# The end of a mixture-of-experts program: waits, gathers and loads behind the last expert

## The chip, the core and the metric

One core of a Trainium2 chip. The time is the device time of one launch in microseconds, the median of three runs. TensorE (PE) does the matmuls, VectorE (DVE) and ScalarE (ACT) the elementwise work, GpSimd (POOL) issues the indirect DMAs and those that add to memory, SyncE (SP) issues the plain loads and stores. Each engine works through its own list of instructions; they meet through semaphores, counters in which a DMA counts 16 when all its data has landed.

## The reference

With x of shape (2, 4096, 512):

```
xn  = layernorm(x)
out = x + attention(xn) + experts(xn)

attention: q, k, v = split(xn @ W_qkv + b_qkv), 16 heads of 32; relu on q and k; both weighted by the cosine and
           the sine of the position; linear attention through k^T v, divided by its norm; then @ W_out + b_out
experts:   probs = softmax(xn @ choice_w^T)                  # 8 experts
           G, I = top_k(probs of each expert, 1024 tokens)   # per batch
           h = silu(xn[I] @ w1[e]);  y = G * (h @ w2[e]);  rows I of the output += y
```

Each of the 8 experts takes 1024 tokens of each of the 2 batches, with w1[e] 512x1024 and w2[e] 1024x512.

## The kernel before

Matmuls are done at more than the plain precision: each operand is split into a high and a low part, and one product is three matmuls (hi·hi, hi·lo, lo·hi; lines 1291 to 1293). The first 960 us or so are the layer norm, attention and routing. They store the normed rows and the router's chances to a scratch tensor in HBM, and write x + bias + attention into the output there.

The rest is the expert stage, and the change is in it alone. It runs over 8 experts (E) and in each over 4 units (UNITS) of 512 token rows, two units for each batch. For a unit:

- GpSimd gathers the rows of the unit to come with 16 indirect DMAs (line 449) and its gains with 4 (line 455), as soon as VectorE has transposed the rows of the present one (`rows_turned`).
- VectorE transposes the rows (line 907), ScalarE takes the high part (`rows_hi`, line 583), VectorE the low part (`rows_lo`, line 914).
- TensorE does the up projection in 8 parts, ScalarE applies silu (line 748), VectorE splits the result (lines 1259 and 1261); then the down projection in 4 tiles of 128 rows. ScalarE scales each tile by the gain into `y` (line 767), and GpSimd scatters it, an indirect DMA that adds 128 rows to the output in HBM (line 546). It counts up `added[b]`.
- ScalarE must not overwrite `y` before the previous unit's scatters have landed. At a unit inside an expert it waits on `added` itself. At the first unit of an expert it waits on `expert_added`, which GpSimd counts up at the end of its loop body, after its own wait for all scatters of batch 1 (lines 551 and 552).
- The weights of the next expert are loaded by SyncE into one raw buffer for w1 (line 357, 4 DMAs) and one for w2 (line 362), each when the split of the present one is done. The split of w1 for the next expert (ScalarE line 579, VectorE line 899) sits in the last unit.
- The token lists of an expert and batch are made by VectorE and TensorE two units ahead; GpSimd copies a new list into `idx`, which the scatters use, at units 1 and 3 (`copy_list`).

`apart(eng)` (line 297) puts a no-op between a wait and the instruction behind it, so that the wait isn't taken into that instruction. GpSimd, SyncE and TensorE run the experts in a hardware loop (`Fori`), in which the values waited for are in registers; ScalarE and VectorE have them written out. All this looks one unit and one expert ahead without an exception at the end: in the eighth expert, w1 and w2 of expert 0 are loaded again, w1 is split again, and in the last unit the rows and gains of unit 0 are gathered, transposed and split again, and `copy_list(0)` runs. Nothing uses them. Behind the loops SyncE waits for those loads and for all stores and scatters, and GpSimd for its scatters and for those gathers (line 553). The Block around the five lists then ends each with a DRAIN and releases them together (in the profile these instructions have line 126).

Of the kernel before, what the change touches and what calls it, by code (L numbers as in the profile page):

```python
# [33 lines left out]
B, L, D = 2, 4096, 512  # L34
H, HD = 16, 32
E, F = 8, 1024
# [3 lines left out]
HPG = P // HD  # L40
KF = F // P
BLK = 512
TPB = BLK // P
# [5 lines left out]
UNITS = B * CAP // BLK  # L49
HALVES = CAP // BLK  # L50
SLOT_TILES = CAP // P
# [6 lines left out]
AHEAD, DMA_AHEAD = 1, 16  # L58
# [60 lines left out]
def build(nc, x, w_qkv, b_qkv, w_out, b_out, choice_w, w1, w2, consts, bits, out, scratch):  # L119
# [6 lines left out]
    with ExitStack() as ctx:  # L126
        def sem(name):
            return ctx.enter_context(nc.semaphore(name))
# [159 lines left out]
        rows_turned, xi_hi_ready, xi_ready = sem("gtr_done"), sem("xi_hi_ready"), sem("xi_ready")  # L288
        up_done, silu_done, h_ready = sem("up_done"), sem("silu_done"), sem("h_ready")
        down_done, y_ready = sem("down_done"), sem("y_ready")  # L290
        added, expert_added = [sem(f"added{b}") for b in range(B)], sem("expert_added")

        block = ctx.enter_context(nc.Block())

        def apart(eng):

            eng.nop(nofuse=True)
# [8 lines left out]
        def _(sp):  # L306

            for signal in (mm_done, kv_done, vv_ready, q_read, k_read, v_read, lg_read, o_raw, otr_done, out_done, fin, list_pe, idx_ready,
                           silu_done, h_ready, down_done, y_ready, expert_added):
                sp.sem_inc(signal, AHEAD)  # L310
            sp.sem_inc(prob_stored, DMA_AHEAD)
            def store_normed(j, s):
# [42 lines left out]
            def load_w1(e):  # L355
                for i in range(HPG):
                    sp.dma_start(w1_raw[i * HD:(i + 1) * HD, :, :],
                                 w1[bass.ds(e, 1), i * P:(i + 1) * P, :].rearrange("e (k p) f -> p (e k) f", p=HD)
                                 ).then_inc(w1_in, 16)

            def load_w2(e):
                sp.dma_start(w2_raw[:, :, :], w2[bass.ds(e, 1), :, :].rearrange("e (k p) d -> p (e k) d", p=P)
                             ).then_inc(w2_in, 16)

            for b in range(B):
# [10 lines left out]
                n = b * NBLK  # L376
# [33 lines left out]
                    sp.wait_ge(q_ready, B * NT)  # L410
                    load_w2(0)

            with sp.Fori(0, E) as e:
                nxt_e = (e + 1) % E
                sp.wait_ge(w1_ready, (e + 1) * KF)
                load_w1(nxt_e)
                sp.wait_ge(w2_ready, (e + 1) * KF)
                load_w2(nxt_e)
            sp.wait_ge(w1_in, HPG * 16 * (E + 1))
            sp.wait_ge(w2_in, 16 * (E + 1))  # L420
            for s in range(2):
                sp.wait_ge(xn_stored[s], 16 * B * NBLK)
            for s in range(RES):
# [7 lines left out]
        def _(pool):  # L431
# [88 lines left out]
            for s in range(RES):  # L520
                pool.wait_ge(out_stored[s], 16 * B * NT // RES)
            pool.wait_ge(prob_stored, DMA_AHEAD + 16 * B)
            with pool.Fori(0, E) as e:
                for u in range(UNITS):
                    b = u // HALVES
                    pool.wait_ge(y_ready, AHEAD + e * (UNITS * TPB) + u * TPB)
                    if u % HALVES == 0:
                        pool.wait_ge(idx_copied, e * B + (b + 1))
                    if u == 1:

                        pool.wait_ge(idx_ready, AHEAD + e * B + 2)
                        apart(pool)
                        copy_list(1)
                    elif u == UNITS - 1:
                        pool.wait_ge(idx_ready, AHEAD + e * B + 3)
                        pool.wait_ge(added[0], (e + 1) * (16 * SLOT_TILES))
                        apart(pool)
                        copy_list(0)
                    pool.wait_ge(rows_turned, (e * UNITS + u + 1) * TPB)
                    apart(pool)  # L540
                    gather((u + 1) % UNITS)

                    for tt in range(TPB):
                        pool.wait_ge(y_ready, AHEAD + e * (UNITS * TPB) + (u * TPB + tt + 1))
                        apart(pool)
                        nc.gpsimd.indirect_dma_start(  # L546
                            of[:, :], bass.IndirectOffsetOnAxis(ap=idx[:, u * TPB + tt:u * TPB + tt + 1], axis=0),
                            y[:, tt, :], None, compute_op=ALU.add).then_inc(added[b], 16)

                pool.wait_ge(added[B - 1], (e + 1) * (16 * SLOT_TILES))  # L550
                pool.sem_inc(expert_added, 1)
            for tt in range(TPB):
                pool.wait_ge(rows_in[tt], 64 * (E * UNITS + 1))
            pool.wait_ge(gain_in[0], 64 * (E * UNITS // 2 + 1))


        @block.scalar
        def _(act):
# [183 lines left out]
            for e in range(E):  # L742
                for u in range(UNITS):
                    n = e * UNITS + u
                    for m in range(KF):
                        act.wait_ge(up_done, n * KF + m + 1)
                        act.wait_ge(h_ready, AHEAD + n * KF + max(m - 1, 0))
                        nc.scalar.activation(hf[:, m % 2, :], ps[:, m % 2, :], ACT.Silu).then_inc(silu_done, 1)  # L748
                        if u == 0:
                            if m == 0:  # L750
                                act.wait_ge(w2_in, (e + 1) * 16)
                                act.wait_ge(down_done, AHEAD + n * TPB)
                            nc.scalar.copy(w2_hi[:, m, :], w2_raw[:, m, :]).then_inc(w2_hi_ready, 1)

                    if u == 0:
                        act.wait_ge(expert_added, AHEAD + e)
                    else:
                        before = u - 1
                        act.wait_ge(added[before // HALVES],
                                    (e * SLOT_TILES + (before % HALVES + 1) * TPB) * 16)  # L760
                    for tt in range(TPB):
                        rows_hi(n + 1, tt)
                        act.wait_ge(down_done, AHEAD + n * TPB + tt + 1)
                        if tt == 0:
                            act.wait_ge(gain_in[u % 2], e * (64 * UNITS // 2) + (u // 2 + 1) * 64)
                        apart(act)
                        nc.scalar.activation(y[:, tt, :], ps[:, 2 + tt % 2, :], ACT.Copy,  # L767
                                             scale=gain[:, u % 2, tt, bass.ds(e, 1)]).then_inc(y_ready, 1)
                        if u == UNITS - 1:
                            if tt == 0:  # L770
                                act.wait_ge(w1_in, (e + 2) * (HPG * 16))
                            for m in (2 * tt, 2 * tt + 1):
                                w1_high(m)
# [3 lines left out]
        def _(dve):  # L777
# [472 lines left out]
            for e in range(E):  # L1250
                for u in range(UNITS):
                    n = e * UNITS + u
                    made, of_b, turn = u % HALVES == 0, (u // HALVES + 1) % B, e * B + (u // HALVES + 1)
                    of_e = e + 1 if of_b == 0 else e
                    for m in range(KF):
                        dve.wait_ge(silu_done, AHEAD + n * KF + m + 1)
                        if m == 0:
                            dve.wait_ge(down_done, AHEAD + n * TPB)
                        me.did(nc.vector.tensor_copy(h_hi[:, m, :], hf[:, m % 2, :]))  # L1259
                        me.wait()  # L1260
                        nc.vector.tensor_tensor(h_lo[:, m, :], hf[:, m % 2, :], h_hi[:, m, :].bitcast(F32),  # L1261
                                                ALU.subtract).then_inc(h_ready, 1)
                        if u == 0:
                            dve.wait_ge(w2_hi_ready, e * KF + m + 1)
                            nc.vector.tensor_tensor(w2_lo[:, m, :], w2_raw[:, m, :], w2_hi[:, m, :].bitcast(F32),
                                                    ALU.subtract).then_inc(w2_ready, 1)
                        if made:
                            if m == 1:
                                list_head(of_e, of_b, turn)
                            elif 2 <= m <= 5:  # L1270
                                list_part(of_e, of_b, turn, m - 2, one_lo[:, m % 2, :, :])
                            elif m == KF - 1:
                                list_tail(of_b, turn, e * B + 1)
                    rows_turn(n + 1, 0)
                    for tt in range(TPB):
                        if tt < TPB - 1:
                            rows_turn(n + 1, tt + 1)
                        rows_lo(n + 1, tt)
                        if made and tt == 1:
                            list_rows(of_b, turn)  # L1280
                        if u == UNITS - 1:
                            for m in (2 * tt, 2 * tt + 1):
                                w1_low(m, e * KF + (KF + m + 1))

# [316 lines left out]
```

## Time and profile before

| | us |
|---|---|
| median of 3 runs (2411.46 to 2414.36) | 2411.73 |
| the profiled execution | 2411.47 |
| its span, first to last instruction | 2409.6 |
| busy in the span: TensorE | 2364.5 |
| VectorE | 1401.0 |
| GpSimd | 1106.8 |
| ScalarE | 839.1 |

Times in the profile are microseconds unless marked ns. A queue's own instructions (names that end in q: waits, branches, DRAIN) are not counted as busy. A matmul's end is modelled, and matmuls overlap, so a busy TensorE is not TensorE at its peak. What a DMA instruction shows as its time on GpSimd is the making of its descriptors; the data lands later, and "to landing" is counted from the start of the instruction. Behind a group in square brackets stands how long its engine was idle before it, and what ended that.

### The profile page before, as it was taken

How to read it: one execution, taken by the hardware profiler on the slowest of the kernel's cores; microseconds unless marked ns; L12 is line 12 of the kernel's file. 1: busy time of each engine (PE TensorE's matmuls, PEld its weight loads, DVE VectorE, ACT ScalarE, POOL GpSimd, SP SyncE). 2: the span in 40 equal slices, each digit the busy share in tenths (PEclk: the TensorE clock that was granted, in tenths of full speed). 3: DMA queues.
4: the chain of work that ended last, by engine and by line, in shares of the span. 5: the costliest groups of instructions: out<-in, count | busy, mean ns of one | idle time of the engine just before them, and what ended most of it. 6: DMA issues, size and time to landing. Idle time of an engine off the chain costs nothing.

```text
span 2409.6 us, 34867 instructions
## 1 busy us (share of the span) xinstructions
PE 2364.5 (98%) x12586; PEld 2006.1 (83%) x12586; DVE 1401.0 (58%) x2730; ACT 839.1 (35%) x1470; POOL 1106.8 (46%) x980
## 2 busy tenths in 40 slices
PE   7999999999999999999999999999999999999997
PEld 6899978888999888888888888888888888888886
DVE  7777788967776888643543543543543544444433
ACT  4455444444454445322322322322223223223222
POOL 2000024400000246666566665665665665765765
PEclk9999999999999999999999999999999999999998
DMA  7555433445453434622522522522523423423322
GB/s 189 168 120 157 121 61 53 56 95 161 121 146 99 76 55 70 152 51 45 121 48 46 119 47 45 120 45 48 120 44 53 116 44 64 104 46 72 94 44 44
DMA packets 128139, 209.66 MB, mean 87 GB/s; under 512 B 28728, under 2 KB 53944, under 8 KB 127808
## 3 DMA queue, kind: packets, MB, share of 16 engines
q0 software_dynamic: 57728, 119.09, 27.6%
q1 hardware_dynamic: 70336, 89.68, 12.9%
q8 instruction: 35, 0.57, 0.1%
q14 instruction: 40, 0.33, 0.0%
HBM read 124.54 MB, written 100.93 MB: 94 GB/s over the span
## 4 chain that ended last, share of the span: by engine, by line
PE 93%; DVE 5%; ACT 1%; issue 1%; DMA 1%; POOL 0%; SPq 0%; DVEq 0%; ACTq 0%; POOLq 0%
PE ps L1291 30%; PE ps L1292 29%; PE ps L1293 29%; PE ps L1387 2%; PE ps L1519 1%; PE ps L1318 1%; DVE work L1229 0%; DVE thr L1141 0%; DVE stats L785 0%; DVE work L1212 0%; DMA xo<-in_L_attn_x_dram 0%; DMA normed_rows<-xo 0%; DVE qT L1004 0%; PE ps L1505 0%; DVE xT_lo L846 0%
## 5 line engine op out<-in xcount | busy, mean ns | idle before, releaser
L449 POOL DMA_INDIRECT rows<-normed_rows,idx_row x528 | 563.7, 1068 | 209.0 <-issue 209.0
L1291 PE MATMUL ps<-xi_hi,w_hi 128*128 128x512 f32 x1024 | 404.3, 395 | 0.0
L1291 PE MATMUL ps<-w_hi,h_hi 128*128 128x512 f32 x1024 | 402.3, 393 | 0.0
L1292 PE MATMUL ps<-xi_lo,w_hi 128*128 128x512 f32 x1024 | 400.4, 391 | 0.0
L1292 PE MATMUL ps<-w_lo,h_hi 128*128 128x512 f32 x1024 | 399.4, 390 | 0.0
L1293 PE MATMUL ps<-w_hi,h_lo 128*128 128x512 f32 x1024 | 399.1, 390 | 0.0
L1293 PE MATMUL ps<-xi_hi,w_lo 128*128 128x512 f32 x1024 | 398.7, 389 | 0.0
L1259 DVE CAST h_hi<-hf 128x512 fp32r<-128x512 f32 x256 | 111.5, 436 | 411.2 <-ACT hf L748 410.9
L546 POOL DMA_INDIRECT out_dram<-y,idx x128 | 221.4, 1730 | 273.1 <-ACT y L767 260.3
L748 ACT ACTIVATE hf<-ps 128x512 f32<-128x512 f32 x256 | 153.1, 598 | 519.4 <-PE ps L1293 519.4
L1293 PE MATMUL ps<-wq_hi,xT_lo 128*128 128x256 f32 (+2 forms) x768 | 246.4, 321 | 0.0
L1291 PE MATMUL ps<-wq_hi,xT_hi 128*128 128x256 f32 (+2 forms) x768 | 246.4, 321 | 0.0
L767 ACT ACTIVATE y<-ps,gain 128x512 f32<-128x512 f32 x128 | 88.1, 689 | 453.6 <-PE ps L1293 453.6
L1292 PE MATMUL ps<-wq_lo,xT_hi 128*128 128x256 f32 (+2 forms) x768 | 245.6, 320 | 0.0
L1293 PEld LDWEIGHTS ps<-xi_hi,w_lo 128*128 128x128 f32 x1024 | 192.7, 188 | 41.0
L1293 PEld LDWEIGHTS ps<-w_hi,h_lo 128*128 128x128 f32 x1024 | 192.5, 188 | 40.5
L1291 PEld LDWEIGHTS ps<-w_hi,h_hi 128*128 128x128 f32 x1024 | 192.4, 188 | 39.1
L1291 PEld LDWEIGHTS ps<-xi_hi,w_hi 128*128 128x128 f32 x1024 | 192.3, 188 | 39.1
L1292 PEld LDWEIGHTS ps<-w_lo,h_hi 128*128 128x128 f32 x1024 | 192.5, 188 | 38.8
L1292 PEld LDWEIGHTS ps<-xi_lo,w_hi 128*128 128x128 f32 x1024 | 192.5, 188 | 38.0
L914 DVE TENSOR_TENSOR xi_lo<-rowsT,xi_hi 128x512 fp32r<-128x512 f32 x132 | 90.4, 685 | 220.0 <-ACT xi_hi L583 216.7
L1261 DVE TENSOR_TENSOR h_lo<-hf,h_hi 128x512 fp32r<-128x512 f32 x256 | 177.9, 695 | 8.8
(174 smaller groups left out, 4217.4 us busy)
## 6 DMA issues: line engine op xcount, KB each, us to landing
w_raw<-in_L_ffn_w_dram SPq DMA_DIRECT2D x36, 512.0 KB, 8.1
w_raw<-in_L_ffn_w_dram SPq DMA_DIRECT2D x9, 2048.0 KB, 9.1
xo<-in_L_attn_x_dram SPq DMA_DIRECT2D x32, 512.0 KB, 4.5
normed_rows<-xo SPq DMA_DIRECT2D x32, 512.0 KB, 4.7
out_dram<-bo POOLq DMA_DIRECT2D x16, 1024.0 KB, 9.2
out_dram<-xo POOLq DMA_DIRECT2D x64, 256.0 KB, 3.9
xn<-normed_rows SPq DMA_DIRECT2D x96, 128.0 KB, 2.4
rows<-normed_rows,idx_row POOLq DMA_INDIRECT x528, 2.6
```

The costliest lines, as they stand in the source:

```text
L449: nc.gpsimd.indirect_dma_start(rows[:, tt, a, :], None, pieces[:, :], bass.IndirectOffsetOnAxis(ap=idx_row[:, b, tile, a:a + 1], axis=0)). ...
L546: nc.gpsimd.indirect_dma_start(of[:, :], bass.IndirectOffsetOnAxis(ap=idx[:, u * TPB + tt:u * TPB + tt + 1], axis=0), y[:, tt, :], None, c ...
L748: nc.scalar.activation(hf[:, m % 2, :], ps[:, m % 2, :], ACT.Silu).then_inc(silu_done, 1)
L767: nc.scalar.activation(y[:, tt, :], ps[:, 2 + tt % 2, :], ACT.Copy, scale=gain[:, u % 2, tt, bass.ds(e, 1)]).then_inc(y_ready, 1)
L914: nc.vector.tensor_tensor(xi_lo[:, :, sl], rowsT[:, tt % 2, :, :], xi_hi[:, :, sl].bitcast(F32), ALU.subtract).then_inc(xi_ready, 1)
L1259: me.did(nc.vector.tensor_copy(h_hi[:, m, :], hf[:, m % 2, :]))
L1261: nc.vector.tensor_tensor(h_lo[:, m, :], hf[:, m % 2, :], h_hi[:, m, :].bitcast(F32), ALU.subtract).then_inc(h_ready, 1)
L1291: nc.tensor.matmul(dst, a_hi, b_hi, start=start, stop=False, skip_group_check=True)
L1292: nc.tensor.matmul(dst, a_hi, b_lo, start=False, stop=False, skip_group_check=True)
L1293: return nc.tensor.matmul(dst, a_lo, b_hi, start=False, stop=stop, skip_group_check=True)
L1318: last = nc.tensor.matmul(ps[:, 4, 16:32], one_lo[:, c % 2, j, :], pay[:, c * 8 + j, :], start=(c == 0 and j == 0), stop=(c == 3 and j == ...
L1387: last = nc.tensor.matmul(ps[:, i // 2, i % 2 * 4 * PW:(i % 2 + 1) * 4 * PW], kk[:, at:at + 2 * PW], vv[:, 2 * at:2 * at + 4 * PW], start= ...
```

## The change

The eighth expert gets exceptions, and one hand-over goes:

- SyncE loads no ninth pair of weights.
- GpSimd's loop runs over seven experts, and the eighth is written out behind it, with constants in its waits. In it the last unit has no `copy_list(0)` and no gathers, and its 16 scatters have no no-op between wait and DMA.
- GpSimd waits for scatters at no expert's end and not at the end of the program; `expert_added` is gone, and ScalarE waits on `added[1]` itself. SyncE's wait for all scatters stays.
- ScalarE and VectorE leave out the rows of unit 32 and the second split of expert 0's w1.

```diff
--- before.py
+++ after.py
@@ -288,7 +288,7 @@
         rows_turned, xi_hi_ready, xi_ready = sem("gtr_done"), sem("xi_hi_ready"), sem("xi_ready")
         up_done, silu_done, h_ready = sem("up_done"), sem("silu_done"), sem("h_ready")
         down_done, y_ready = sem("down_done"), sem("y_ready")
-        added, expert_added = [sem(f"added{b}") for b in range(B)], sem("expert_added")
+        added = [sem(f"added{b}") for b in range(B)]
 
         block = ctx.enter_context(nc.Block())
 
@@ -306,7 +306,7 @@
         def _(sp):
 
             for signal in (mm_done, kv_done, vv_ready, q_read, k_read, v_read, lg_read, o_raw, otr_done, out_done, fin, list_pe, idx_ready,
-                           silu_done, h_ready, down_done, y_ready, expert_added):
+                           silu_done, h_ready, down_done, y_ready):
                 sp.sem_inc(signal, AHEAD)
             sp.sem_inc(prob_stored, DMA_AHEAD)
             def store_normed(j, s):
@@ -410,14 +410,13 @@
                     sp.wait_ge(q_ready, B * NT)
                     load_w2(0)
 
-            with sp.Fori(0, E) as e:
-                nxt_e = (e + 1) % E
+            with sp.Fori(0, E - 1) as e:
                 sp.wait_ge(w1_ready, (e + 1) * KF)
-                load_w1(nxt_e)
+                load_w1(e + 1)
                 sp.wait_ge(w2_ready, (e + 1) * KF)
-                load_w2(nxt_e)
-            sp.wait_ge(w1_in, HPG * 16 * (E + 1))
-            sp.wait_ge(w2_in, 16 * (E + 1))
+                load_w2(e + 1)
+            sp.wait_ge(w1_in, HPG * 16 * E)
+            sp.wait_ge(w2_in, 16 * E)
             for s in range(2):
                 sp.wait_ge(xn_stored[s], 16 * B * NBLK)
             for s in range(RES):
@@ -520,7 +519,7 @@
             for s in range(RES):
                 pool.wait_ge(out_stored[s], 16 * B * NT // RES)
             pool.wait_ge(prob_stored, DMA_AHEAD + 16 * B)
-            with pool.Fori(0, E) as e:
+            def expert(e, last):
                 for u in range(UNITS):
                     b = u // HALVES
                     pool.wait_ge(y_ready, AHEAD + e * (UNITS * TPB) + u * TPB)
@@ -531,27 +530,27 @@
                         pool.wait_ge(idx_ready, AHEAD + e * B + 2)
                         apart(pool)
                         copy_list(1)
-                    elif u == UNITS - 1:
+                    elif u == UNITS - 1 and not last:
                         pool.wait_ge(idx_ready, AHEAD + e * B + 3)
                         pool.wait_ge(added[0], (e + 1) * (16 * SLOT_TILES))
                         apart(pool)
                         copy_list(0)
-                    pool.wait_ge(rows_turned, (e * UNITS + u + 1) * TPB)
-                    apart(pool)
-                    gather((u + 1) % UNITS)
+                    if u < UNITS - 1 or not last:
+                        pool.wait_ge(rows_turned, (e * UNITS + u + 1) * TPB)
+                        apart(pool)
+                        gather((u + 1) % UNITS)
 
                     for tt in range(TPB):
                         pool.wait_ge(y_ready, AHEAD + e * (UNITS * TPB) + (u * TPB + tt + 1))
-                        apart(pool)
+                        if not last:
+                            apart(pool)
                         nc.gpsimd.indirect_dma_start(
                             of[:, :], bass.IndirectOffsetOnAxis(ap=idx[:, u * TPB + tt:u * TPB + tt + 1], axis=0),
                             y[:, tt, :], None, compute_op=ALU.add).then_inc(added[b], 16)
 
-                pool.wait_ge(added[B - 1], (e + 1) * (16 * SLOT_TILES))
-                pool.sem_inc(expert_added, 1)
-            for tt in range(TPB):
-                pool.wait_ge(rows_in[tt], 64 * (E * UNITS + 1))
-            pool.wait_ge(gain_in[0], 64 * (E * UNITS // 2 + 1))
+            with pool.Fori(0, E - 1) as e:
+                expert(e, False)
+            expert(E - 1, True)
 
 
         @block.scalar
@@ -752,21 +751,22 @@
                                 act.wait_ge(down_done, AHEAD + n * TPB)
                             nc.scalar.copy(w2_hi[:, m, :], w2_raw[:, m, :]).then_inc(w2_hi_ready, 1)
 
-                    if u == 0:
-                        act.wait_ge(expert_added, AHEAD + e)
-                    else:
+                    if u == 0 and e > 0:
+                        act.wait_ge(added[B - 1], e * (16 * SLOT_TILES))
+                    elif u > 0:
                         before = u - 1
                         act.wait_ge(added[before // HALVES],
                                     (e * SLOT_TILES + (before % HALVES + 1) * TPB) * 16)
                     for tt in range(TPB):
-                        rows_hi(n + 1, tt)
+                        if n + 1 < E * UNITS:
+                            rows_hi(n + 1, tt)
                         act.wait_ge(down_done, AHEAD + n * TPB + tt + 1)
                         if tt == 0:
                             act.wait_ge(gain_in[u % 2], e * (64 * UNITS // 2) + (u // 2 + 1) * 64)
                         apart(act)
                         nc.scalar.activation(y[:, tt, :], ps[:, 2 + tt % 2, :], ACT.Copy,
                                              scale=gain[:, u % 2, tt, bass.ds(e, 1)]).then_inc(y_ready, 1)
-                        if u == UNITS - 1:
+                        if u == UNITS - 1 and e < E - 1:
                             if tt == 0:
                                 act.wait_ge(w1_in, (e + 2) * (HPG * 16))
                             for m in (2 * tt, 2 * tt + 1):
@@ -1271,14 +1271,17 @@
                                 list_part(of_e, of_b, turn, m - 2, one_lo[:, m % 2, :, :])
                             elif m == KF - 1:
                                 list_tail(of_b, turn, e * B + 1)
-                    rows_turn(n + 1, 0)
+                    more = n + 1 < E * UNITS
+                    if more:
+                        rows_turn(n + 1, 0)
                     for tt in range(TPB):
-                        if tt < TPB - 1:
+                        if more and tt < TPB - 1:
                             rows_turn(n + 1, tt + 1)
-                        rows_lo(n + 1, tt)
+                        if more:
+                            rows_lo(n + 1, tt)
                         if made and tt == 1:
                             list_rows(of_b, turn)
-                        if u == UNITS - 1:
+                        if u == UNITS - 1 and e < E - 1:
                             for m in (2 * tt, 2 * tt + 1):
                                 w1_low(m, e * KF + (KF + m + 1))
```

## Rows read from the trace of the kernel before

**Rows 1.** The page's part 4, the chain of waits by engine, share of the span.

```profile
PE 93%; DVE 5%; ACT 1%; issue 1%; DMA 1%; POOL 0%; SPq 0%; DVEq 0%; ACTq 0%; POOLq 0%
```

**Rows 2.** Windows, first and last expert: stretch, length, busy us (instructions), clock, DMA share, GB/s.

```profile
966.00:1144.00 178.00, 178.00 (x842) 145.81 (x841) 86.78 (x157) 47.13 (x79) 116.18 (x102) 1.00 0.38 80
...
2216.00:2395.00 179.00, 178.38 (x840) 146.05 (x838) 79.62 (x138) 47.48 (x81) 113.85 (x98) 1.00 0.36 72
```

**Rows 3.** Timeline after the last matmuls: start us, us, engine, line, operation [idle before <-releaser].

```profile
2393.99 0.39 PE L1293 MATMUL ps<-w_hi,h_lo 128*128 128x512 f32 x1
2394.47 0.69 ACT L767 ACTIVATE y<-ps,gain 128x512 f32<-128x512 f32 x1 [3.20 <-PE ps L1293]
2395.06 1.12 ACT L579 CAST w_hi<-w_raw 128x512 fp32r<-128x512 f32 x2
2395.70 1.29 DVE L899 TENSOR_TENSOR w_lo<-w_raw,w_hi 128x512 fp32r<-128x512 f32 x2 [3.54 <-ACT w_hi L579]
2395.92 1.90 POOL L546 DMA_INDIRECT out_dram<-y,idx  x1 [3.52 <-ACT y L767]
```

**Rows 4.** One source line, L126, queues' own instructions: ns min/median/max, first to last start.

```profile
L126 POOLq EVENT_SEMAPHORE  x2: 17/17/17, 2409.5 to 2409.5; - x2
...
L126 ACTq DRAIN  x1: 1672/1672/1672, 2394.5 to 2394.5; - x1
L126 DVEq DRAIN  x1: 814/814/814, 2396.2 to 2396.2; - x1
...
L126 POOLq DRAIN  x1: 7912/7912/7912, 2401.5 to 2401.5; - x1
```

**Rows 5.** Line L546 from 2395 us on: the last scatter's landing, from its issue.

```profile
DMA to landing us min/median/max: 5.0/5.0/5.0
```

**Rows 6.** Lines L427 (SyncE's last waits) and L553 (GpSimd's last wait).

```profile
L427 SPq EVENT_SEMAPHORE  x1: 28/28/28, 2400.9 to 2400.9; - x1
...
L553 POOLq EVENT_SEMAPHORE  x1: 43/43/43, 2401.2 to 2401.2; - x1
```

**Rows 7.** Windows: the end of the span after the landing (columns as in rows 2).

```profile
2400.90:2409.60 8.70, 0.00 (x0) 0.00 (x0) 0.00 (x0) 0.00 (x0) 0.00 (x0) 0.50 0.00 0
```

**Rows 8.** Line L1590, the start of the program, GpSimd (columns as in rows 4).

```profile
L1590 POOLq DRAIN  x1: 184/184/184, 0.3 to 0.3; - x1
...
L1590 POOL MEMSET const-uint8-127<- x1: 117/117/117, 0.3 to 0.3; 128x1 uint8 x1
```

**Rows 9.** Line L297, the no-op of apart(), on GpSimd's queue.

```profile
L297 POOLq EVENT_SEMAPHORE  x176: 17/17/17, 978.8 to 2395.2; - x176
```

**Rows 10.** Timeline of stage 2's end: ScalarE finishes a tile, GpSimd's DMA adds it.

```profile
971.25 0.59 ACT L738 COPY xo<-ps 128x512 f32<-128x512 f32 x1 [0.68 <-DMA out_dram<-xo]
...
972.13 0.90 POOL L502 DMA_DIRECT2D out_dram<-xo  x1 [1.78 <-ACT xo L738]
```

**Rows 11.** Lines L357 and L362, the loads of w1 and w2, SyncE's queue.

```profile
L357 SPq DMA_DIRECT2D w_raw<-in_L_ffn_w_dram x36: 311/317/686, 807.4 to 2221.2; - x36
...
L362 SPq DMA_DIRECT2D w_raw<-in_L_ffn_w_dram x9: 385/390/390, 961.4 to 2242.2; - x9
```

**Rows 12.** Timeline of GpSimd in the last unit.

```profile
2381.82 1.61 POOL L546 DMA_INDIRECT out_dram<-y,idx  x1 [0.30 <-issue]
2385.09 1.93 POOL L546 DMA_INDIRECT out_dram<-y,idx  x1 [1.66 <-ACT y L767]
```

**Rows 13.** Timeline of GpSimd where the seventh expert ends.

```profile
2218.36 1.89 POOL L546 DMA_INDIRECT out_dram<-y,idx  x1 [3.54 <-ACT y L767]
2227.47 1.96 POOL L449 DMA_INDIRECT rows<-normed_rows,idx_row  x1 [7.21 <-issue]
```

**Rows 14.** Line L546 from 2215 to 2229 us: that scatter's landing.

```profile
DMA to landing us min/median/max: 7.6/7.6/7.6
```

**Rows 15.** Timeline of VectorE, without and beside GpSimd's gathers.

```profile
2220.67 0.69 DVE L1261 TENSOR_TENSOR h_lo<-hf,h_hi 128x512 fp32r<-128x512 f32 x1
...
2228.91 0.69 DVE L1261 TENSOR_TENSOR h_lo<-hf,h_hi 128x512 fp32r<-128x512 f32 x1
```

## The prediction, made before the changed kernel was run

> **What bounds the kernel now.** I read the chain of waits first: 93% of the span is TensorE [rows 1]. Then the expert stage by expert, one stretch for each: in all eight TensorE is busy for the whole stretch (178.00 of 178.00 in the first, 178.38 of 179.00 in the last, which ends after TensorE does), at a granted clock of 1.00 [rows 2]. So nothing that another engine does in this stage is waited for by TensorE, and what the change can move lies behind the last matmul. I then read the end of the program by engine. The last recorded matmul runs to about 2394.4, ScalarE scales y from 2394.47 to 2395.16, GpSimd issues the last scatter from 2395.92 to 2397.82 [rows 3]. The span ends at 2409.6, 11.8 us later, with no engine busy. The queues' own instructions fill that tail. ScalarE's DRAIN starts at 2394.5 and ends at 2396.2, and VectorE's starts at 2396.2 and ends at 2397.0: both end with the last instruction of their engine. GpSimd's starts at 2401.5 and takes 7.912 us, to 2409.4; the semaphores that release all engines stand at 2409.5 [rows 4]. So the end is: last y, last scatter, its landing, GpSimd's waits, GpSimd's DRAIN. The landing is 5.0 us after the issue, at 2400.9 [rows 5]; at 2400.9 SyncE's wait on the same scatters is over too, and GpSimd's last wait, on gathers long landed, stands at 2401.2 [rows 6]. In the 8.7 us from 2400.90 on no DMA engine moves anything [rows 7]: the drain isn't waiting for data then, it takes 7.9 us of its own.
>
> **The change part by part.** The sum is made on the profiled execution, 2411.47 us with a span of 2409.6; the 1.9 us around the span stay. The median, 2411.73, lies 0.26 above it, and the gain is taken from the median.
>
> 1. GpSimd's wait for the last scatters, the increment behind it, the loop's last branch and the waits on the ninth expert's gathers go. Before, the drain starts at 2401.5; now its sequencer reaches it as soon as the scatter is handed over. What the drain then costs is not in the trace for this case (scatters in flight). Bounds: it needs its 7.9 us after GpSimd's own last instruction, or it needs all of them after the landing (gain only the 0.6 us of sequencer work between 2400.9 and 2401.5), or it costs next to nothing: the same engine's drain at the program's start, behind four memsets, took 184 ns and ended with them [rows 8]. With that last one SyncE's landing sets the end, and the gain is 2409.4 - 2400.9 = 8.5 us. I take the first. It is nearest to rows 4 and 8: no drain in the trace ends earlier than its engine's work, and this one ran its 7.9 us with the DMA engines at rest, so most of it should be work that does not need the landing. Drain start moves from 2401.5 to 2397.8: 3.7 us.
>
> 2. In the last expert the no-op between wait and scatter goes, and the waits compare with constants. The no-op takes 17 ns [rows 9], but the scatter starts 0.76 us after y is done (2395.16 to 2395.92). Of a GpSimd DMA with a constant wait and no no-op, the nearest rows are the ones that add stage 2's output: xo is done at 971.84 and the DMA starts at 972.13, 0.29 us [rows 10]. So 0.76 - 0.29 = 0.47 us; bounds 0 (an indirect DMA may need the 0.7 anyway) and 0.47. I take 0.45. All later steps of the tail, the landing too, move with it.
>
> 3. The ninth expert. SyncE issues 36 w1 and 9 w2 loads, the last of them at 2221.2 and 2242.2 [rows 11]: 4 of 0.5 MB and one of 2 MB go. They land over 140 us before the end and TensorE waits for nothing there: 0. In the last unit 20 gathers go. They held back that unit's first scatter, but the second one starts with the waiting pattern again (2385.09, after 1.66 us idle) [rows 12], so by then GpSimd had caught up: 0. ScalarE's casts of w1 and VectorE's subtractions run to 2396.18 and 2396.99 [rows 3] and go with the transposes; both engines drained before GpSimd. If GpSimd's tail shrank by all 8.5 us, the next thing late would be the landing at 2400.5, still behind these two: 0. TensorE's stretches are full with such loads in each of them [rows 2], so fewer neighbours give it nothing.
>
> 4. GpSimd no longer waits at each expert's end either, and ScalarE waits on the scatters itself, 8 activations later, when they are long in. At such an end the last scatter runs from 2218.36 to 2220.25, and the next gather starts at 2227.47, after 7.21 us idle [rows 13], because beside the weight load that scatter takes 7.6 us to land [rows 14]. The landing, at 2226.0, was 5.7 of those 7.2 us, so these gathers start about 6 us sooner, seven times. They were not late, so no gain; the cost is what they disturb. VectorE's TENSOR_TENSOR takes 0.69 us while GpSimd idles and 0.69 us beside its gathers [rows 15]: 0.
>
> 5. GpSimd's last expert is written out, so its program is longer. It has some 65 us of idle time in each expert (113.85 us busy of 179 in the last) [rows 2]: 0.
>
> Sum: the last scatter starts at 2395.92 - 0.45 = 2395.47 and ends at 2397.37; drain to 2405.3 instead of 2409.4; gain 4.1 us (3.7 + 0.45). 2411.73 - 4.1 = **2407.6 us**, 0.17% less.
>
> The Trainium skill has two rules on this instruction. VectorE: DVE Perf Modes (The DRAIN you can't avoid) says that the drains around a program take about 12 ns on every engine. By it GpSimd's drain would be free, SyncE's wait on the same scatters would end the program either way, and edits 1 and 2 would give only 0.6 + 0.45 = 1.1 us. The trace disagrees with it: 7.912 us for GpSimd [rows 4]. PSUM — Partial Sum Buffer (Engine vs sequencer instructions) says "drain waits for the engine to go fully idle"; if a scatter in flight counts against idle, this is the first rival.
>
> **The rivals.**
> First, the drain is tied to the landing: it finds the scatter in flight, waits, and does its 7.9 us then. For it: the last scatter is in flight from 2397.4 to 2400.5, and the 7.9 us, absent at the start, seem to belong to DMAs. Against: nothing moves during it. Gain 0.6 + 0.45 = 1.1: 2410.6.
> Second, the drain's 7.9 us run beside the scatter's own 1.9 us of descriptor work, counted from when the sequencer reaches it, about 2395.5. For it: ScalarE's drain starts right at 2394.5, ahead of its engine's end. Against: that drain still ends with its engine. Drain to 2403.4, gain 6.0: 2405.7. With a drain that costs almost nothing it would be 2411.7 - 8.5 - 0.45 = 2402.8, which only the start's 184 ns speaks for.
> Third, on the other side: at the seven expert boundaries the earlier gathers run in the stretch where VectorE is fullest (w2's subtractions and the list marks), their descriptor writing slows it, and TensorE is late into the down projection. To undo the 4.1 us it needs 0.6 us of stall for each boundary, and 1.3 us each, 4.1 + 4.8 = 8.9 us over seven, to come out over 0.2% slower: 2416.6. Against it: the equal 0.69 us [rows 15], and TensorE's full stretches with such gathers in each.
> Fourth, nothing changes: the drain's end is set by something that starts neither with the scatter nor with the wait. 2411.7.
>
> **How the numbers follow.** This kernel's time can be told from no change at about 0.2%, 4.8 us. Chances: forecast 0.52, drain tied to the landing 0.22, drain beside the scatter or shorter 0.17, slower boundaries 0.04, nothing 0.05. The forecast stays within 0.2% unless its terms are a fifth larger, for which I give 0.05 of its 0.52. Faster by over 0.2%: 0.17 + 0.05 = 0.22; slower by over 0.2%: 0.03; within: 0.75. The range reaches from just below the second rival (2405.7) to above the first and the fourth: 2405.0 to 2411.8. Left out are the nearly free drain and a real slowdown.
>
> **What would show it.** GpSimd's DRAIN starts near 2395.5 and ends near 2405.3, and the span ends 0.2 us behind it; SyncE's wait on the scatters ends near 2400.5, before it. The step on the no-op is right if the last scatter starts 0.3 us after y, wrong if 0.7. The gap before the first gather of each later expert falls from 7.2 us to 1.5 or less, or it shows that something else than the wait filled it. TensorE's stretches stay full; its last matmul stays at 2394.4. I am wrong if the drain ends later than 8.2 us behind the last scatter's end (the first rival has it at 11), earlier than 7.5 (the second), or if the last matmul has moved by over 0.5 us (the third).

## The result, and the profile after

| | before | after |
|---|---|---|
| median, us (8 runs each) | 2412.1 | 2405.9 |
| ratio, 95% interval | | 0.9972 (0.9961 to 0.9982) |
| the profiled execution, us | 2411.47 | 2405.74 |
| its span, us | 2409.6 | 2403.9 |

The change makes the kernel 0.28% faster: 6.7 us by the ratio, 6.2 us by the two medians and 5.7 us by the two profiled executions. The forecast was 2407.6. For the experiments further below: beside the last four kernels of their table the kernel before took 2534 us instead of 2412, at a mean granted clock of 0.98 instead of 1.00, so of those four the ratio and the tails are used and not the times.

The chain of waits of the changed kernel, by engine, has the same head as [rows 1]:

```profile
PE 93%; DVE 5%; issue 1%; DMA 1%; ACT 1%; POOLq 0%; POOL 0%; SPq 0%; DVEq 0%; ACTq 0%
```

The windows of its last expert and of the end behind the landing (columns as in [rows 2]):

```profile
2216.00:2395.00 179.00, 178.67 (x841) 146.15 (x840) 70.36 (x124) 41.92 (x71) 87.80 (x77) 1.00 0.27 43
2400.50:2403.90 3.40, 0.00 (x0) 0.00 (x0) 0.00 (x0) 0.00 (x0) 0.00 (x0) 0.50 0.01 2
```

TensorE is as full as before, and VectorE, ScalarE and GpSimd have less to do. The timeline of the end, which answers to [rows 3]:

```profile
2394.28 0.39 PE L1296 MATMUL ps<-w_hi,h_lo 128*128 128x512 f32 x1
2394.76 0.69 ACT L767 ACTIVATE y<-ps,gain 128x512 f32<-128x512 f32 x1 [4.75 <-PE ps L1296]
2395.73 1.55 POOL L547 DMA_INDIRECT out_dram<-y,idx  x1 [3.89 <-ACT y L767]
```

The queues' own instructions at the end, which answer to [rows 4] (ns min/median/max, first to last start):

```profile
L126 POOLq EVENT_SEMAPHORE  x2: 17/17/17, 2403.7 to 2403.8; - x2
L126 DVEq DRAIN  x1: 732/732/732, 2374.0 to 2374.0; - x1
...
L126 ACTq DRAIN  x1: 699/699/699, 2394.8 to 2394.8; - x1
L126 POOLq DRAIN  x1: 8164/8164/8164, 2395.5 to 2395.5; - x1
...
L126 SPq DRAIN  x1: 7/7/7, 2401.1 to 2401.1; - x1
```

GpSimd's DRAIN now starts at 2395.5 and reads 8.164 us, to 2403.66; it is still the last thing. SyncE's wait for the scatters was over at 2400.5, and its own DRAIN at 2401.1. What the changed kernel saved is best read from the end of the last y, since the spans of its executions differ by over 3 us among themselves (2402.0 to 2405.5). Where in an execution these differences arise is not shown, since one execution of each kernel was profiled; that it is ahead of the last y is likely, since two kernels with the same end have tails of 8.45 and 8.46 us below. Before, the DRAIN ended 14.25 us behind y (2395.16 to 2409.41), now 8.21 us (2395.45 to 2403.66): 6.04 us less.

The gap at an expert's end [rows 13] is gone: GpSimd's first gather of the last expert follows 0.30 us behind the scatter.

```profile
2218.66 1.90 POOL L547 DMA_INDIRECT out_dram<-y,idx  x1 [3.53 <-ACT y L767]
2220.85 1.02 POOL L448 DMA_INDIRECT rows<-normed_rows,idx_row  x1 [0.30 <-issue]
```

### The profile page after: what moved, and what is told of

Read it like the earlier page. It is cut to its first block, busy times and chain, and to the rows that moved or that the text cites. A ratio compares the mean times of both kernels' runs of the same rounds, so it can differ in the third digit from the quotient of the medians.

```text
span 2403.9 us, 34741 instructions
## 1 busy us (share of the span) xinstructions
PE 2364.3 (98%) x12586; PEld 2004.2 (83%) x12586; DVE 1390.2 (58%) x2714; ACT 832.8 (35%) x1458; POOL 1080.5 (45%) x959
## 3 DMA queue, kind: packets, MB, share of 16 engines
q1 hardware_dynamic: 68720, 85.48, 12.3%
## 4 chain that ended last, share of the span: by engine, by line
PE 93%; DVE 5%; issue 1%; DMA 1%; ACT 1%; POOLq 0%; POOL 0%; SPq 0%; DVEq 0%; ACTq 0%
PE ps L1294 30%; PE ps L1295 29%; PE ps L1296 29%; PE ps L1390 2%; PE ps L1522 1%; PE ps L1321 1%; DVE work L1229 0%; DVE qT L1004 0%; DMA normed_rows<-xo 0%; DVE thr L1141 0%; DMA xo<-in_L_attn_x_dram 0%; DVE stats L785 0%; DVE work L1212 0%; DVE xT_lo L846 0%; PE ps L1508 0%
## 5 line engine op out<-in xcount | busy, mean ns | idle before, releaser
L448 POOL DMA_INDIRECT rows<-normed_rows,idx_row x512 | 542.6, 1060 | 156.7 <-issue 156.7
```

The lines of the kernel that those rows point to most:

```text
L448: nc.gpsimd.indirect_dma_start(rows[:, tt, a, :], None, pieces[:, :], bass.IndirectOffsetOnAxis(ap=idx_row[:, b, tile, a:a + 1], axis=0)). ...
```

## The experiments

The tail below is the time from the end of the last y to the end of the span, in the one profiled execution of each kernel. Where the end is the same it agrees within 0.1 us (8.45 and 8.46 for the changed kernel and boundary_waits), so it tells apart what the ratios, with intervals of some 2 us to either side, can't. Where the table has no ratio, the kernel was executed once.

| kernel | ratio to before (interval) | tail, us | GpSimd's last DRAIN, us |
|---|---|---|---|
| before | 1 | 14.44 | 7.912 |
| changed | 0.9972 (0.9961 to 0.9982) | 8.45 | 8.164 |
| drain_late | 0.9993 (0.9984 to 1.0002) | 11.79 | 6.279 |
| noop_kept | 0.9979 (0.9970 to 0.9988) | 9.03 | 8.214 |
| ninth_only | 0.9993 (0.9984 to 1.0002) | 12.33 | 6.279 |
| boundary_waits | 0.9981 (0.9972 to 0.9990) | 8.46 | 8.157 |
| drain_2_6_later | one execution | 8.83 | 6.279 |
| drains_early | one execution | 5.93 | 5.274 |
| no_drain | 0.9964 (0.9951 to 0.9978) | 5.86 | none |
| before_no_drain | 0.9968 (0.9956 to 0.9980) | 6.69 | none |
| one_drain | 0.9961 (0.9947 to 0.9975) | 5.81 | 5.173 |
| one_drain_late | one execution | 5.85 | 0.380 |
| drain_unit1 | one execution | 7.47 | 7.176 |
| twenty_more_late | one execution | 13.38 | 7.912 |

Theory A is the forecast's: the drain is a fixed 7.9 to 8.2 us.

**drain_late**, the wait alone put back:

```
             expert(E - 1, True)
+            pool.wait_ge(added[B - 1], E * (16 * SLOT_TILES))
```

> The changed kernel with one wait put back: behind its last scatter GpSimd waits for it to land, and only then reaches its DRAIN. Theory A (the drain is a fixed 7.9 to 8.2 us, counted from when GpSimd's sequencer reaches it, and in the changed kernel it ran beside the scatter and its landing): the drain starts near 2401.2 instead of 2395.5, takes 7.9, the span ends near 2409.2 (2403.9 + 5.3) and the time is 2411.2 where the changed kernel has 2405.9. Theory C (a good part of the 6 us came from something else, the earlier gathers or the missing ninth expert): the wait costs clearly less than 5 us, 2 to 4.

The drain, reached at 2400.9, took only 6.279 us; the tail grew by 3.34 us, not 5.3.

```profile
L126 POOLq DRAIN  x1: 6279/6279/6279, 2400.9 to 2400.9; - x1
...
L126 SPq DRAIN  x1: 7/7/7, 2401.3 to 2401.3; - x1
```

So the wait is worth 3.3 us, and the drain is no fixed 7.9 us: with the same wait ahead of it as before, it is 1.63 us shorter. Theory C has the number (2 to 4 us), and one of its two sources: the rest came from the missing ninth expert, as the runs below show, not from the earlier gathers.

**noop_kept**, with `apart(pool)` unconditional in front of the scatter:

> The changed kernel with the no-op between wait and scatter kept in the last expert. Theory A: the scatter starts 0.7 us after y instead of 0.3, the DRAIN is reached about 0.45 us later, and the span and the time are 0.45 us longer (2406.35). Rival: the no-op's delay is hidden in the scatter's own 1.6 to 1.9 us, and the end stays where it is (2405.9). A single span can't tell 0.45 us by itself, since spans of the changed kernel differ by over 3 us; the distance from the end of y to the end of the DRAIN can: 8.21 us without the no-op, 8.65 with it.

y ends at 2393.57, the scatter starts 0.76 us later as before, and the tail is 9.03 us against 8.45.

```profile
2392.88 0.69 ACT L766 ACTIVATE y<-ps,gain 128x512 f32<-128x512 f32 x1 [4.75 <-PE ps L1295]
2394.33 1.55 POOL L546 DMA_INDIRECT out_dram<-y,idx  x1 [3.89 <-ACT y L766]
```

The no-op costs 0.48 us at this place (0.76 against 0.28); the tail says 0.58. The ratios are too wide to show it.

**ninth_only**, the no-ops as above and at the end of every expert

```
+                pool.wait_ge(added[B - 1], (e + 1) * (16 * SLOT_TILES))
```

> Only the ninth expert's work is left out: no loads, gathers, transposes and splits for it; GpSimd waits for its scatters at the end of every expert, the last too, and keeps its no-ops. Theory A: the same time as the kernel before (2412.1), drain from about 2401.4 for 7.9 us. Theory C: the missing 4 MB of loads and the emptier last unit are worth something by themselves, 1 us or more.

```profile
L126 POOLq DRAIN  x1: 6279/6279/6279, 2402.5 to 2402.5; - x1
```

The tail is 2.11 us shorter than before. Of these, 1.63 are in the drain (6.279 again). Another 0.4 lie between the landing and the drain: where the increment, the loop's branch and the waits on the ninth expert's gathers stood, 0.6 us become 0.2 (2400.9 to 2401.5 before, 2402.3 to 2402.5 here). The last scatter takes 1.55 us instead of 1.90, but as the drain comes behind the landing here, only 0.1 of that counts: it lands 4.9 us after its start instead of 5.0.

```profile
L426 SPq EVENT_SEMAPHORE  x2: 27/28/28, 2313.6 to 2402.3; - x2
```

Its ratio says 1.7 us, with an interval that takes in none. So to leave out the ninth expert is worth some 2 us, against theory A, and they are gained at the end, not in the last unit.

**boundary_waits**, the same line under `if not last:`, no-ops as in the change:

> The changed kernel, but GpSimd waits for its scatters at the end of the first seven experts, so the gathers behind them start as late as before; at the end of the program it doesn't wait. Theory A: the same time as the changed kernel (2405.9), since TensorE waits for nothing in the expert stage. Theory C: the earlier gathers gave part of the gain, and this kernel is slower by 1 us or more.

Tail 8.46 us against 8.45, so at the end the earlier gathers are worth nothing. Its median, 2407.06, is 1.2 us above the changed kernel's, which is what theory C asked for, but the two intervals (0.9972 to 0.9990, 0.9961 to 0.9982) overlap and the two kernels weren't timed in one series. Five kernels were timed in one series, and the median less the tail tells what lies ahead of the last y. With these waits it is 2397.3 us in the kernel before, 2397.9 in ninth_only and 2398.6 in boundary_waits; without them it is 2397.4 in noop_kept and 2398.1 in drain_late. So no clear effect of the waits shows. About 1 us isn't excluded, but TensorE has no idle time in the expert stage that they could have shortened.

**drain_2_6_later**, behind the last y on ScalarE, and behind the last scatter on GpSimd:

```
+                            for i in range(2):
+                                act.wait_ge(y_ready, AHEAD + E * UNITS * TPB + i)
+                                nc.scalar.copy(hf[:, :, :], ps[:, 2:4, :]).then_inc(y_ready, 1)
...
+            pool.wait_ge(y_ready, AHEAD + E * UNITS * TPB + 2)
```

> The changed kernel, but GpSimd reaches its DRAIN about 2.6 us later: behind the last y ScalarE does two more activations of 128x1024 into a free buffer, and GpSimd waits for the second one behind its last scatter. The scatter itself is not moved and is still in flight when the drain starts. Theory A (fixed from when it is reached): the drain takes 8 us from its start and the tail from the end of y to the end of the drain grows from 8.21 us to about 10.7. Theory B (tied to the landing: it ends about 3.2 us behind it) and theory B2 (about 6.4 us behind the end of the scatter's descriptor work): the tail stays at 8.2 us and the DRAIN reads 5.5 us.

Neither the 2.5 us more of theory A nor the unchanged tail of B and B2 came. The two activations were over 2.1 us behind y, the drain was reached at 2398.5, took 6.279 us, and the tail is only 0.4 us longer.

```profile
2396.26 2.06 ACT L774 COPY hf<-ps 128x1024 f32<-128x1024 f32 x2
2396.44 1.55 POOL L547 DMA_INDIRECT out_dram<-y,idx  x1 [3.89 <-ACT y L768]
```

```profile
L126 POOLq DRAIN  x1: 6279/6279/6279, 2398.5 to 2398.5; - x1
```

The scatter's descriptor work ended at 2397.99, and it landed at 2401.1. The drain did its 6.28 us from 2398.5 on, 2.6 of them in the scatter's flight. So it needs 6.28 us behind whichever is later, its being reached or the end of GpSimd's own work, and the landing, which is over before that, doesn't hold it here. In the changed kernel that is 2397.28 + 0.1 + 6.28 = 2403.66: the 8.164 us that the profile shows there are 1.8 us of waiting for the scatter's descriptors and 6.3 us of work.

**drains_early**, `nc.gpsimd.drain()` at three places (GpSimd's lines 438, 511 and 546 of that kernel):

> The changed kernel with three more DRAINs in GpSimd's list where it has time: before its first DMA of all (near 15 us), behind its first two DMAs, and in the idle stretch before the last unit's first scatter, directly behind the scatters of the unit before. Theory A1 (a fixed price once software DMAs have been used, whatever came since the last drain): about 0.2 us for the first, about 8 us for each of the others, and the last one of the program stays at 8.2 us. Theory A2 (a price for the DMAs issued since the last drain, as a clean-up): the drain behind two DMAs is short, the one in the last expert takes about 8 us, and the one at the end, with only 4 scatters since, is far shorter than 8 us; the span would then end near the landing, 2401.

```profile
L438 POOLq DRAIN  x1: 562/562/562, 13.9 to 13.9; - x1
...
L511 POOLq DRAIN  x1: 12441/12441/12441, 52.3 to 52.3; - x1
...
L546 POOLq DRAIN  x1: 8064/8064/8064, 2352.0 to 2352.0; - x1
...
L126 POOLq DRAIN  x1: 5274/5274/5274, 2395.5 to 2395.5; - x1
```

The first, ahead of all DMAs of GpSimd, ends with the cast before it (13.95 to 14.42; the drain to 14.5): it costs nothing. The second, behind two DMAs, takes 12.441 us, to 64.7: theory A2 said short, but the second of these DMAs was issued at 52.36 and took 12.3 us to land, at 64.66. So this drain waited for what was in flight. The third is 8.064 us, of which 6.3 lie behind the scatter's descriptors. The last one ends at 2400.8, 0.2 us behind the landing (2395.74 + 4.8), 2.9 us sooner than in the changed kernel. The landing of the second DMA, from its issue:

```profile
DMA to landing us min/median/max: 12.3/12.3/12.3
```

So the drain has two parts, the landing and a work for earlier DMAs, and an early drain takes the second away from the end.

**no_drain** and **before_no_drain**, `nc.Block(no_gpsimd_drain=True)`:

> The changed kernel whose Block closes with semaphores alone and without GpSimd's DRAIN (the other engines drain as before; SyncE's wait for all scatters stays). Theory A: the drain was the last thing by 2.8 us (2403.66 against 2401.1), so the span ends at about 2401.2 and the time falls by 2.6 us, to 2403.3. Rival: the price only moves out of the drain into what follows it, and the time stays.

> The kernel before with only GpSimd's DRAIN left out of the Block's end. Theory A: the end is the landing and GpSimd's waits behind it, 2401.6 instead of 2409.6: the time falls by 8 us, to 2404.1, that is by more than the whole change gave, and the changed kernel without a drain is only about 1 us faster than this one (the no-op and GpSimd's last waits). Rival (the 8 us belong to the program's end whatever the drain): no difference from before.

The end of no_drain, where no GpSimd DRAIN stands between SyncE's and the release:

```profile
L126 SPq EVENT_SEMAPHORE  x2: 17/17/17, 2400.8 to 2401.0; - x2
L126 POOLq EVENT_SEMAPHORE  x2: 17/17/17, 2400.9 to 2401.0; - x2
...
L126 SPq DRAIN  x1: 7/7/7, 2400.8 to 2400.8; - x1
```

Both as theory A has them: tails of 5.86 us (2.59 less than the changed kernel) and 6.69 us (7.75 less than before). With the drain gone, the kernel before is within 0.83 us of the changed one: the no-op's 0.48, and 0.4 in the landing, which follows 5.1 us behind the start of a scatter of 1.90 us and 4.7 us behind the start of one of 1.55; the queues' last instructions are 0.1 shorter before. So 5.2 of the 6.0 us went through this one instruction.

**one_drain**, the early drain in the last unit alone:

```
                         gather((u + 1) % UNITS)
+                    else:
+                        nc.gpsimd.drain()
```

> The changed kernel with one DRAIN more, in GpSimd's 26 us of idle time before the last unit's first scatter. Theory A2 (a drain goes through the software DMAs issued since the last one, and besides waits for the last landing): the early drain takes about 8.1 us unseen, the last one has 4 scatters left and ends 0.2 us behind the landing, as in the kernel with three early drains (5.27 us from its start). The span is then that of the kernel without any GpSimd drain, and the time is about 2403.4, 2.5 us less than the changed kernel and 8 to 9 less than before. Theory A1 (a fixed price): 2405.9, as the changed kernel.

```profile
L543 POOLq DRAIN  x1: 8044/8044/8044, 2470.3 to 2470.3; - x1
...
L126 POOLq DRAIN  x1: 5173/5173/5173, 2513.8 to 2513.8; - x1
...
L126 SPq DRAIN  x1: 7/7/7, 2519.4 to 2519.4; - x1
```

0.9961 (0.9947 to 0.9975), tail 5.81 us: faster than before by 0.39%, and its tail is 2.64 us shorter than the changed kernel's. The early drain takes its 8 us at 2470, where GpSimd has nothing else to do until 2497. The last one ends 0.2 us behind the last scatter's landing, which is now the end. By their intervals it and no_drain can't be told apart from the changed kernel, by their tails they can.

**one_drain_late**, with drain_late's wait as well:

> As the kernel with one early drain, and GpSimd waits for its last scatter's landing before it reaches the last DRAIN, which so has nothing to wait for. Theory A2 at 82 ns for each DMA since the last drain (7.912 us before against 6.279 us in the kernels without the ninth expert's 20 gathers: 1.633 us / 20): 4 scatters cost about 0.3 us. Theory A1: 6.3 us, as in the other kernels with this wait.

```profile
L126 POOLq DRAIN  x1: 380/380/380, 2506.2 to 2506.2; - x1
```

0.380 us for 4 scatters, 95 ns each if nothing in it is fixed. What a drain leaves to the next one is far less than the 6.279 us without it.

**twenty_more_late**, 20 gathers of unit 0's pieces and gains in the last unit's idle time, and drain_late's wait:

> The changed kernel with 20 more gathers in the last unit, into buffers that nobody reads any more (the same number as the ninth expert's before, but nothing is transposed or split), and with the wait for the last landing ahead of the last DRAIN. Theory A2: 20 x 82 ns more than the 6.279 us of the kernel with that wait alone: 7.9 us, as before. If the 1.6 us between 7.912 and 6.279 came from anything else (the longer GpSimd loop, SyncE's ninth loads, VectorE's and ScalarE's work), it stays at 6.3.

```profile
L126 POOLq DRAIN  x1: 7912/7912/7912, 2530.1 to 2530.1; - x1
```

7.912 us, to the nanosecond what the kernel before had. These 20 gathers, and neither the loads nor the other engines' work, made the 1.633 us: 82 ns for each. They had long landed when the drain began. The last scatter takes 1.55 us here, though the gathers are back, so they didn't cause the 1.90 us before.

**drain_unit1**, the early drain two units sooner, at unit 1 of the last expert:

> The changed kernel with one DRAIN more, at unit 1 of the last expert before its gathers, so that 40 gathers and 12 scatters come between it and the last DRAIN. Theory A2: 52 x 82 ns = 4.25 us behind the end of the last scatter's descriptor work, that is a last DRAIN of 1.9 + 4.25 = 6.1 us from its start, between the changed kernel's 8.16 and the 5.27 with 4 scatters. Theory A3 (only what was issued in the last few tens of us counts): 5.3 or 8.2.

```profile
L126 POOLq DRAIN  x1: 7176/7176/7176, 2493.5 to 2493.5; - x1
...
L126 SPq DRAIN  x1: 7/7/7, 2499.0 to 2499.0; - x1
```

7.176 us, from 2493.5 to 2500.7. The last scatter's descriptors ended at 2495.25, so 5.4 us lie behind them, where 52 DMAs at 82 ns give 4.3. A3's two values, 5.3 and 8.2, are both off by a microsecond or more, and the price does lie between those of 4 DMAs and of the changed kernel, but 1.1 us of it isn't explained: 104 ns for each of the 52, against 95 for the 4 scatters and 82 for the 20 gathers. So the price of a DMA isn't constant, or they don't all count alike. Nor can the price be 82 ns for each DMA since the program's start: the changed kernel issues 864 of them, and 6.28 us pay for 77. As the drain has no more than that to do, earlier DMAs must drop out of the reckoning on the way; how and when, these runs don't show.

## Why the prediction was right, and where it was not

The time, 2405.9, lies in the range, and the sign was right; the gain was forecast as 4.1 us and is 6.0 in the tail. In its own steps, all from the end of y to the end of the drain:

| step | forecast, us | measured, us |
|---|---|---|
| the wait goes, the drain follows the scatter's descriptors | 3.7 | 3.58 |
| the no-op goes | 0.45 | 0.48 |
| the ninth expert, in the drain (20 gathers fewer) | 0 | 1.63 |
| the ninth expert, in the last scatter (1.90 to 1.55) | 0 | 0.35 |
| sum | 4.1 | 6.04 |

The no-op's 0.48 us and the 1.63 us of the gathers are measured by runs of their own. The first row is what the others leave of 6.04, and it agrees with the trace: before, the drain started 3.68 us behind the end of the scatter's descriptors, now its work starts 0.1 us behind it. The 0.35 us of the scatter count in full because the drain in the changed kernel starts its work behind the descriptors and not behind the landing.

- Bounds: right. The last y, its scatter, and GpSimd's DRAIN set the end, and TensorE waits for nothing in the expert stage, before or after.
- Step 1: right, though it was a choice between bounds, since the trace before held no drain with a scatter in flight. The drain needs its time behind GpSimd's own last work and works while the scatter is in flight (drain_2_6_later).
- Step 2: right. The nearest row, 0.29 us without a no-op, holds for the indirect DMA (0.28).
- Step 3 failed, by 1.98 us. It asked of each transfer and operation left out whether something waited for it in the last unit, where nothing did. But the 20 gathers came back as 1.63 us in the drain, and VectorE's w1 split ran in the first 1.1 us of the last scatter. "This one ran its 7.9 us with the DMA engines at rest, so most of it should be work" was the right reading; the next question, work on what, and does the change alter its amount, was not asked.
- Step 4: right in that the tail doesn't move and the gap closes (7.21 to 0.30). Step 5: the longer list shows no cost.
- The rivals. The drain tied to the landing (2410.6) was wrong: it doesn't put its work off until then. That it isn't over before the landing is right, and shows where the work is small (one_drain, 0.2 us behind). The drain counted from when it is reached has the right time, 2405.7, for a wrong reason: reached 2.3 us behind y instead of 0.05 (drain_2_6_later), it didn't move the end by 2.3 us but by 0.4, and its length fell from 8.16 to 6.28. The prediction's own sign of being wrong, a drain that ends sooner than 7.5 us behind the last scatter's end, came true: it was 6.4 us. It was meant to speak for this rival, but what made it short was the missing gathers. The nearly free drain's end (tail 5.9) is what one_drain and no_drain have.
- The chances: within 0.2% had 0.75 and faster by more had 0.22; it came out 0.28% faster, with an interval (0.18 to 0.39%) over that line for the most part. The forecast by itself gave the terms too little room upward, since it held step 3 at an exact 0.

On the two rules of the Trainium skill: VectorE: DVE Perf Modes (The DRAIN you can't avoid) gives some 12 ns for the drains of the runtime's own preamble and postamble. The drains here end the kernel's Block, which is another place than the page speaks of, so the prediction stretched it by taking it for this one; SyncE's takes 7 ns, GpSimd's 0.38 to 7.91 us when all its DMAs have landed. PSUM — Partial Sum Buffer (Engine vs sequencer instructions) says that "drain waits for the engine to go fully idle". The drain behind two DMAs agrees with it if transfers in flight count, 12.441 us to 0.1 us behind the landing; of the work for DMAs that landed long ago it says nothing.

## What to carry to other kernels

Read a program's end from the last compute instruction on, the queues' own instructions included: here one DRAIN of an engine that was 46% busy was the last 8 us. A drain on GpSimd costs more the more DMAs it has issued of late, so put a drain where GpSimd is idle anyway, a few DMAs before the end (4 here; with 52 the tail was still 1.7 us longer); then the last transfer's landing is the end, and a wait ahead of the last drain costs next to nothing (5.85 against 5.81 us). Work that is left out because "nothing waits for it" can still be paid for later, in whatever goes through all that was issued.

## What the runs showed of the hardware that was not expected

- GpSimd's DRAIN has a price for DMAs that GpSimd issued earlier, though all have landed: 7.912 and 6.279 us, 20 gathers apart, which is 82 ns for each; 0.380 us with 4 scatters since the drain before. It also doesn't end before the last one has landed (12.441 us behind two).
- A scatter's descriptor work mostly takes 1.8 to 1.9 us if it starts while VectorE is in a TENSOR_TENSOR, and 1.55 to 1.61 us if not. In the trace of the kernel before, 60 of the 70 scatters of the first kind and none of the 58 of the second took over 1.8 us. Both kinds are in the last expert, the first in noop_kept, where the VectorE instruction starts 0.22 us earlier, the second in the changed kernel, where it starts 0.26 us later:

```profile
2345.15 0.69 DVE L913 TENSOR_TENSOR xi_lo<-rowsT,xi_hi 128x512 fp32r<-128x512 f32 x1 [4.75 <-ACT xi_hi L581]
...
2345.37 1.90 POOL L546 DMA_INDIRECT out_dram<-y,idx  x1 [3.51 <-ACT y L766]
```

```profile
2346.77 1.56 POOL L547 DMA_INDIRECT out_dram<-y,idx  x1 [3.86 <-ACT y L767]
...
2347.03 0.69 DVE L914 TENSOR_TENSOR xi_lo<-rowsT,xi_hi 128x512 fp32r<-128x512 f32 x1 [4.75 <-ACT xi_hi L582]
```

The Trainium skill's GPSIMD Engine Reference (Key points) has GpSimd share its SBUF interfaces with VectorE, with contention when a VectorE instruction has two SBUF inputs, as this one has; these rows agree, with 0.35 us. That the second scatter is not slowed, though the whole TENSOR_TENSOR runs beside it, speaks for the start being what counts.
